# A vision-transformer block: matmuls of the attention step in another order, and image loads on another queue

## The reference

```python
qkv = x @ w_attn + b_attn
att = jnp.einsum('bhqd,bhkd->bhqk', q, k) * (1.0 / math.sqrt(HS))
att = jnp.where(causal[None, None, :, :], att, -jnp.inf)
att = jax.nn.softmax(att, axis=-1)
y = jnp.einsum('bhqk,bhkd->bhqd', att, v)
h = _layernorm(h + y @ w_proj + b_proj)
```

## Time and profile before

| | us |
|---|---|
| median of 3 runs (lowest to highest) | 2457.37 (2453.13 to 2463.67) |
| the profiled execution | 2454.87 |
| its span, first to last instruction | 2453.1 |
| PE busy in the span | 2181.2 (89%) |
| DVE, ACT, POOL busy | 1597.5, 1095.1, 1337.1 |
| attention block ends near | 1440 |

### The profile page before, as it was taken

How to read it: one execution, slowest core, us unless ns; L and a number is a source line. 1 busy time by engine, 2 the same in 40 slices (tenths; PEclk the granted TensorE clock), 3 DMA queues, 4 the chain that set the end, 5 groups by cost and what they waited for, 6 DMA issues and landing times. The chain is left out here.

```text
span 2453.1 us, 47733 instructions
## 1 busy us (share of the span) xinstructions
PE 2181.2 (89%) x14772; PEld 2102.4 (86%) x14772; DVE 1597.5 (65%) x4464; ACT 1095.1 (45%) x2873; POOL 1337.1 (55%) x2133
## 2 busy tenths in 40 slices
PE   4688999999999999999999929999999999999970
PEld 3688988889999989888988819999999999999970
DVE  4366676777767777677777736666666666666646
ACT  2243444444444444444444405455545454545537
POOL 3234665656566757576755653454545454544443
PEclk8799998999999999999999959999999999999985
DMA  6876454454545454545453223311111111111337
GB/s 203 246 234 177 115 145 110 118 137 113 137 108 140 108 134 107 132 105 135 107 134 84 52 73 73 77 31 52 29 49 32 49 32 49 31 26 26 52 65 281
DMA packets 188285, 251.80 MB, mean 103 GB/s; under 512 B 59567, under 2 KB 144685, under 8 KB 183040
## 3 DMA queue, kind: packets, MB, share of 16 engines
q1 hardware_dynamic: 105424, 157.22, 23.7%
q10 hardware_dynamic: 31792, 80.37, 11.7%
q0 software_dynamic: 50944, 12.63, 4.0%
HBM read 145.04 MB, written 125.29 MB: 110 GB/s over the span
## 5 line engine op out<-in xcount | busy, mean ns | idle before, releaser
L1054 POOL DMA_INDIRECT x_tokens<-yout,target x240 | 377.8, 1574 | 449.3 <-DVE yout L1217 417.9
L646 PE MATMUL Y<-p,vp 128*102 128x198 f32 x1536 | 413.9, 354 | 15.7 <-POOL p L428 7.0
L1232 DVE TENSOR_TENSOR a<-UP,gate 128x384 f32<-128x384 f32 x320 | 178.4, 558 | 215.0 <-ACT gate L1178 211.0
L406 POOL TENSOR_TENSOR x_lo<-x,x_hi 128x396 fp32r<-128x396 f32 x192 | 211.6, 1104 | 188.8 <-ACT x_hi L461 185.0
L441 POOL DMA_INDIRECT expert_lists<-pay,slot x256 | 283.3, 1107 | 54.6 <-issue 54.6
L492 ACT ACTIVATE p<-ST 128x396 f32<-128x396 f32 x384 | 191.2, 498 | 256.2 <-PE ST L625 245.3
L1133 PE MATMUL Y<-w,a_hi 128*128 128x384 f32 x960 | 303.7, 354 | 2.0 <-DVE a_lo L1222 2.0
L1178 ACT ACTIVATE gate<-GT 128x384 f32<-128x384 f32 x320 | 157.5, 492 | 294.5 <-PE UP L1120 294.5
L648 PEld LDWEIGHTS Y<-p,vp 70*102 70x102 f32 x1536 | 265.7, 173 | 1.7
L140 POOL TENSOR_TENSOR word_p<-word_p 1x1 f32<-1x1 f32 x416 | 93.7, 225 | 313.4 <-ACT p L494 301.8
L807 DVE TENSOR_REDUCE rm<-S 128x2 f32<-128x256 f32 x384 | 161.3, 420 | 136.4 <-PE S L638 128.9
(11 more groups left out here) (186 smaller groups left out, 6416.4 us busy)
## 6 DMA issues: line engine op xcount, KB each, us to landing
x<-in_xt ACTq DMA_DIRECT2D x30, 1188.0 KB
q<-qk_features SPq DMA_DIRECT2D x384, 74.2 KB
k<-qk_features SPq DMA_DIRECT2D x192, 148.5 KB
expert_lists<-blank ACTq DMA_DIRECT2D x16, 1455.0 KB, 9.2
rows<-expert_lists SPq DMA_DIRECT2D x80, 291.0 KB
qk_features<-qk_hi SPq DMA_DIRECT2D x96, 198.0 KB, 2.6
qk_features<-qk_lo SPq DMA_DIRECT2D x96, 198.0 KB, 3.1
e_raw<-in_wexp SPq DMA_DIRECT2D x8, 1408.0 KB, 6.8
```

The lines of the kernel that those rows point to most:

```text
L406: pool.tensor_tensor(x_lo[:, t], x[:, t], x_hi[:, t].bitcast(F32), ALU.subtract)\
L646: pe.matmul(Y[0:VW1, 0:TI], v0, p32[b][:, hh, 0:TI], start=(h % 6 == 0), stop=False)
L1054: pool.indirect_dma_start(d["x1"][:, :], bass.IndirectOffsetOnAxis(ap=target[cc % 4][:, t:t + 1], axis=0), yout[q][:], None, bounds_check= ...
L1232: dve.tensor_tensor(a32[m % 2][:], UP[m % 2][:, 0:TILE3], gate[m % 2][:], ALU.mult)\
```

## The change

Two edits, both in the attention block.

The first writes TensorE's step in another order. The turned scores and the scores are no longer two groups in a row: first `ST[0]`, then the wait for the maxima and `S[0]` of the first head, then `ST[1]`, then `S[1]`, and the second head's `S[0]` and `S[1]`; the small mask (L638) goes ahead of the large one (L636), and the signal `s_s` comes from the large one. In `values` the two short matmuls stand together, and a long one always comes last. The second edit issues the load of `x` from SP, at step 8 behind the token store and ahead of the spread of step 9, in place of ACT.

```diff
--- before.py
+++ after.py
@@ SP
+                    if s == 8 and "E" in stages and (not isinstance(i, int) or i + 2 < NPAIR):
+                        if not isinstance(i, int):
+                            sp.wait_ge(s_qset, 5)
+                        sp.wait_ge(s_xlo, (i + 2) * KT)
+                        sp.dma_start(x[:], d["xt"][i + 2]).then_inc(s_x, 16)
@@ ACT
-                    if s == 8 and "E" in stages and (not isinstance(i, int) or i + 2 < NPAIR):
-
-                        act.wait_ge(s_xlo, (i + 2) * KT)
-                        act.dma_start(x[:], d["xt"][i + 2]).then_inc(s_x, 16)
@@ PE, values
+                if opens:
+                    first_keys(*heads[0], True, False)
+                for hh, h in heads:
+                    last_keys(hh, h)
+                if not opens:
+                    first_keys(*heads[0], False, False)
+                first_keys(*heads[1], False, j % 3 == 2).then_inc(s_pv, 1)
@@ PE, step
-                        turned_scores(im, j, q[pr], k[pr]).then_inc(s_st, 1)
-                    if 2 in stages:
+                        turned_first(tim, tj, q[pr], k[pr])
+                    if scored:
 ...
                         wait(pe, s_m, n)
-                        scores(s // 6, s % 6, q[1 - par], k[1 - par]).then_inc(s_s, 1)
+                        scores_first(im, j, 0, qs, ks)
+                    if turned:
+                        turned_second(tim, tj, q[pr], k[pr])
+                    if scored:
+                        scores_second(im, j, 0, qs, ks)
+                        scores_first(im, j, 1, qs, ks)
+                        scores_second(im, j, 1, qs, ks)
+                        mask_scores()
```

More of the change, by code:

```diff
@@ L618, in _, with turned_first @@
                     embed(0, ft, k0)
-            def turned_scores(im, j, qt, kt):
+            def turned_first(im, j, qt, kt):
                 rows = slice(0, ROWS_QK + 1)
@@ L624, in turned_scores, with turned_second @@
                           start=True, stop=True)
-                return pe.matmul(ST[1][0:T1, 0:2 * T1], kt[rows, im, j, P:TI], qt[rows, im, :, j, P:TI],
-                                 start=True, stop=True)
-            def scores(im, j, qt, kt):
-                rows = slice(0, ROWS_QK)
[L631 to L636, removed]
+            def turned_second(im, j, qt, kt):
+                rows = slice(0, ROWS_QK + 1)
+                pe.matmul(ST[1][0:T1, 0:2 * T1], kt[rows, im, j, P:TI], qt[rows, im, :, j, P:TI],
+                          start=True, stop=True).then_inc(s_st, 1)
@@ new lines, in scores_first, with scores_second @@
+            def scores_first(im, j, b, qt, kt):
+                rows = slice(0, ROWS_QK)
+                pe.matmul(S[0][:, b * P:(b + 1) * P], qt[rows, im, b, j, 0:P],
+                          kt[rows, im, j, 0:P], start=(b == 0), stop=False)
+            def scores_second(im, j, b, qt, kt):
+                rows = slice(0, ROWS_QK)
+                pe.matmul(S[1][0:T1, b * TI:(b + 1) * TI], qt[rows, im, b, j, P:TI],
+                          kt[rows, im, j, :], start=(b == 0), stop=False)
@@ L637, in scores, with mask_scores, first_keys @@
+            def mask_scores():
                 own = S[1][0:T1, 0:TP].rearrange("p (h c) -> p h c", h=2)[:, :, P:TI]
-                return pe.matmul(own, identb[0:T1, 0:T1], repeat(maskb[0:T1, 0:T1], 2), start=False, stop=True)
+                pe.matmul(own, identb[0:T1, 0:T1], repeat(maskb[0:T1, 0:T1], 2), start=False, stop=True)
+                pe.matmul(S[0][:, 0:2 * P], identb, repeat(maskb, 2), start=False, stop=True).then_inc(s_s, 1)
             def values(im, j, b):
-                for hh in range(2):
-                    h = 2 * j + hh
+                heads = [(hh, 2 * j + hh) for hh in range(2)]
+                opens = j % 3 == 0
+                def first_keys(hh, h, start, stop):
@@ L644, in values, with last_keys @@
                     v0 = vp[im][:, h * VW1:(h + 1) * VW1]
+                    return pe.matmul(Y[0:VW1, 0:TI], v0, p32[b][:, hh, 0:TI], start=start, stop=stop)
+                def last_keys(hh, h):
                     v1 = vp[im][0:T1, (NH + h) * VW1:(NH + h + 1) * VW1]
[L646 to L649, removed]
@@ L650, in values @@
-                return mm
+                    pe.matmul(Y[0:VW1, P:TI], v1, p32[b][0:T1, hh, TI:TI + T1], start=False, stop=False)
+                if opens:
[5 more added lines that the diff above has]
+                first_keys(*heads[1], False, j % 3 == 2).then_inc(s_pv, 1)
             def body(i, turn, par, stages):
@@ L655, in body @@
                     n = (i - 1) * STEPS + s
-                    if is_step(n - LAG):
-                        im, j, back = score_step(s)
+                    turned, scored = is_step(n - LAG), 2 in stages
+                    if turned:
+                        tim, tj, back = score_step(s)
                         pr = parity(par, back)
-                        if j == 0:
-                            pe.wait_ge(s_nmd[im], (i - back + 1) * 16)
+                        if tj == 0:
+                            pe.wait_ge(s_nmd[tim], (i - back + 1) * 16)
                         wait(pe, s_exp, n - LAG)
-                        turned_scores(im, j, q[pr], k[pr]).then_inc(s_st, 1)
-                    if 2 in stages:
+                        turned_first(tim, tj, q[pr], k[pr])
+                    if scored:
+                        im, j, qs, ks = s // 6, s % 6, q[1 - par], k[1 - par]
                         if s % 6 == 0:
@@ L677, in body @@
                         pe.wait_ge(s_mask, m * 2 + 2)
-                        values(im, j, (s + 1) % 3).then_inc(s_pv, 1)
+                        values(im, j, (s + 1) % 3)
                     for name in g.pieces(s):
```

## The result

| | before | after |
|---|---|---|
| median (lowest to highest), us | 2460.52 (2453.13 to 2470.17) | 2422.28 (2422.11 to 2428.91) |
| ratio, 95% interval | | 0.9867 (0.9836 to 0.9899) |
| span of the profiled execution, us | 2453.1 | 2420.5 |

The change is worth 1.3%, 38 us by the medians and 33 us by the two profiled executions. The direction was right. The forecast of 2378 was 44 us too low, and the time lies outside the range (2356 to 2403).

A forecast was written before the change was run, and what follows sets the result against it. PE was taken to bound the attention block, lengthened by idle gaps, a lowered clock and matmuls spaced beyond their streams. Stalls 44 + clock 19 + order 14 = 77 us off 2454.9 gave 2378, range 2356 to 2403.

The forecast's parts named there:

- Stalls, 44 us: Attention block: with x off ACT's queue, rb comes in time and PE's stalls behind it go; gain 44 us.
- the upper bound of 11.6: Worst case for rb's landing: 11.6 us after issue as at present, if shared engines and not the queue hold it.
- rival C: rb stays late because it shares engines with x and the second spread; 2441, or 2400 with half the stall; chance 0.13.
- Clock, 19 us: PE's stretches at 1.2 GHz in the attention block, some 58 us, go with the stalls; gain 19 us.
- Clock falls without stalls: Sign against the forecast: clock drops that stay without stalls, which would leave 19 us in place.
- Order, 14 us: PE's reordered step and `values` in the attention block save 0.49 us a body over some 29 bodies, 14 us.
- Start, 0 taken within -4 and +6: First two bodies: SP issues x later than ACT did, but q and k land sooner; between -4 and +6 us, counted as 0.
- B: Matmul order in the attention block is worth nothing, as loads run ahead or PE waits for DVE; 2392; chance 0.17.
- D: x comes late on SP's queue and holds ACT's `x_hi` at step 0; slower, 2495 at 21 us; chance 0.04.
- E: Better case: all weight loads hidden, lowered stretches worth half their time, 6 us at the start; 2352; chance 0.08.

The follow-up runs named there:

- no_x: Changed kernel without the loads of x from the third pair on and without ACT's wait for them; 2363.38 us, ratio 0.9618.
- x_in_six: Changed kernel with x loaded as six transfers of 198 KB from the same place in SP's queue; 2367.62 us, ratio 0.9637.
- spread_held: Changed kernel with the second spread of q and k moved to step 11 and held there by a wait on TensorE's progress; 2369.12 us, ratio 0.9641.
- queue_only: Kernel before with only the load of x moved to SP's queue, old matmul order; 2436.89 us, ratio 0.9913.
- x_in_eight_rows: Changed kernel with x cut by partitions into eight transfers of 16 rows of 9504 bytes; 2398.08 us, ratio 0.9719.
- order_only: Changed kernel with the load of x back on ACT's queue, so only the matmul order is new; 2462.61 us, ratio 1.0021.
- six_old_order: Kernel with x in six transfers on SP and the old order of the matmuls; 2385.5 us, ratio 0.9669.
- x_after_spread: Changed kernel with x, in one transfer, issued at step 10 behind the second spread on SP; 2383.24 us, ratio 0.9689.
- six_old_again: Second run, in another job, of x in six transfers on SP with the old matmul order; 2381.64 us, ratio 0.9676.

## Why the prediction was right or wrong

**Stalls, 44 us: this step failed.** It said of `rb`'s landing "I take 7 to 9, nearer the first, since the row beside it has the same traffic and lacks only `x`". DVE read it after 11.1 us in the mean, near the upper bound of 11.6 (12.2 in the turn shown; 11.4 in the mean before). The reasoning took the row without `x` for the row with `x` on another queue. The earlier trace rows could only say what `rb` needs when no `x` is in flight; that ACT's queue was the holder was not in it. Nor was it in the wait coming once a body, for the `rb` behind `x`: that fits shared engines as well, since `x` is in flight only then. Of the 44 us the term gave 7.2 by the waits from 140 to 1300 us (50.9 to 43.7), and 3.4 over the same 26 bodies (46.5 to 43.1), where PE's idle time as a whole did not fall. The runs showed in its place that nearly all of one large transfer is served ahead of `rb`'s first row from either queue (117 and 122 of 128 rows have started; 4.2 us, against 4.7 on the same queue and 1.5 without `x`), and that the rest of `rb` is then slow beside the second spread (last row at 9.7 us, at 5.8 with the spread held back). This is the mechanism of rival C, to which 0.13 was given, half of it near 2400 and the range ending at 2403. The measured 2422 lies between its two prices, 2400 and 2441. That the bound 11.6 was kept in the text, and not in the range, was the second fault: "28 x 0.7 = 20 us less" for an `rb` at 10.9 stood there already. (Even that was too mild. 0.7 us off each of 28 stalls is a gain of 20 us in place of 44, so 24 less.)

**Clock, 19 us: the mechanism was right, the size hung on the stalls.** The time at 1.2 GHz fell by 13.6 us, which at the prediction's 0.33 is 4.5 us (over the same 26 bodies by 10.2 us, some 4 us). Where the stalls went (`no_x`, `x_in_six`, `spread_held`) it fell to 3.4, 6.8 and 3.4 us. Clock falls without stalls, one of the things that would have shown it wrong, did not appear to any size there.

**Order, 14 us: right, and most of what the change gave.** The step reads 0.76. Second halves take 20.73 (forecast 20.7, before 20.89), first halves without a stall 18.12 (forecast 18.2). Without stalls the order is worth 0.47 us a body, where 0.49 was worked out. In the change as made it was paid although the stalls stayed: 0.6 us a body before what the waits take, some 15 of the 18.6 us of the full bodies. What it is worth still depends on the rest of the kernel. By itself, with `x` on ACT's queue, it was worth nothing (1.0021): longer waits and more time at 1.2 GHz took it back. The two parts apart come to 16 us by their ratios (21 and -5), and both together to 33. The sum took the three terms as independent, and these runs do not bear that out.

**Start, 0 taken within -4 and +6: mis-sized.** It measured 11.4 us in the profiled executions, and 9.1 in `queue_only`. The size is loose: the marker stands at 173 to 179 us in the three kernels with `x` on ACT's queue, and from 160.5 to 169.9 in the nine with `x` at step 8 on SP or without it, leaving out `x_in_eight_rows`. Before the change ACT issued the next `x` at 90.24 us, and the last spread of that body started on SP at 91.01; PE then waited for its operands:

```profile
106.82 0.41 PE L632 MATMUL S<-k,q 96*70 96x198 f32 x1 [6.89 <-issue]
```

After it SP issues the spread first and `x` behind it:

```profile
91.08 2.90 SPq L347 DMA_DIRECT2D q<-qk_features  x6
94.03 1.77 SPq L355 DMA_DIRECT2D k<-qk_features  x3
95.84 0.42 SPq L384 DMA_DIRECT2D x<-in_xt  x1
```

The wait of 6.89 us is gone, though PE waits 3.09 us for `nm` a little earlier instead (at 90.88). The direction of this ("lets q and k land sooner") was in the prediction, without a row to size it by; before the change the share of the DMA engines reads 0.98 to 1.11 in each 5 us from 80 to 110 us. That this wait makes most of the gain at the start is read from the trace and was not tested apart.

**Rivals.** B, the order worth nothing: true of `order_only`, false in the kernel after and where PE is not stalled. D, `x` late on SP's queue: not in the full bodies. What the prediction set against it holds: before the change the last row of `x` had ended 10.2 us or less after its issue and at least 2.0 us ahead of that of the `rb` behind it, in 28 turns of 28. In the first ones ACT's longest wait for `x` grew from 8.2 to 18.3 us, and the start still gained. E did not come in, but `x_in_six` with 2366 to 2368 lies between E and the forecast.

**The prices were sound and the cause was not.** For "`rb` in time" the sum gave 2378 with nothing at the start; the three kernels with the new order in which `rb` is in time and the start is unharmed measured 2363 to 2369, and the start can be the difference. PE's waits for the maxima fell to 12.1 to 14.5 us there (forecast about 8). The full bodies alone, in the profiled executions, agree more closely. With the old order and `rb` in time (`six_old_order`) they take 64.9 us less than before, against 63 forecast for stalls and clock; the new order takes another 12.8 off 26 bodies, against 0.49 x 26 = 12.7.

## What to carry to other kernels

Moving a large load to another engine's queue did not protect the small transfer that DVE was waiting for (70.7 us of waits before, 58.3 after). What did (3.4 us or less in `x_in_six`, `spread_held` and `x_after_spread`) was to cut the large load into small transfers on the other queue, to hold back what is issued behind it, or to issue it later. A row in which the large load is absent tells what the small one needs, not what the queue costs; ask for a row with both in flight on different queues before pricing such a change, and if there is none, keep the bad bound in the range. Before adding up the terms of a change, ask whether each is paid without the others, and run the parts apart: here one part alone was worth nothing, the other 21 us, and both 33. And compare traces over the same bodies and not over the same microseconds, or a shift of the start is counted as a gain of the loop.

## What the runs showed of the hardware

- One transfer of 1188 KB (128 rows of 9504 bytes) delays the first row of a transfer issued 0.1 to 0.6 us later on another queue from 1.4 or 1.5 to 4.2 us; cut in six it delays it to 1.9, cut in eight to 1.7. The same queue adds only 0.5 us to that when `x` is one transfer (4.7), but 4.4 when it is six (6.3).
- Two harmless neighbours add up to a harmful one: with `x` but the spread held the last row starts at 5.8 us, with the spread but `x` behind it at 3.7, and with both at 9.7.
- Six issues in a row hold ScalarE for 2.71 us ahead of its next instruction. On SP, which computes nothing here, the 3.90 us of six issues cost nothing that could be seen; they put the second spread 3.5 us behind `rb`, and a delay of the spread alone helped too (`spread_held`: last row at 5.8 us for 9.7).
- A half body with a stretch at 1.2 GHz costs 0.36 to 0.39 us more for each us of it: one with 6.83 us of it in the kernel after takes 23.60 us, 3.15 of them idle, where such a half takes 18.00 at full clock.
- The time is less even in the kernel before: 17 runs of it in one job lie between 2442.65 and 2470.05, four of `x_in_six` in the same job between 2364.26 and 2367.92. That the stalls make it so is not shown: four runs of the kernel after, which stalls too, lie within 6.8 us, and four of `six_old_again`, which does not, within 14.6.
